# Two layers of gated cross-attention: the first layer's keys and queries as a seven-part block product

## The reference, cut to what matters

```python
x = _rmsnorm(hidden_states, ln_weight)
h_q = (x @ w_q.T).reshape(b, lq, H, DH)                     # H, DH = 32, 128; D = 512
h_k = (key_value_states @ w_k.T).reshape(b, lk, H, DH)
h_v = (key_value_states @ w_v.T).reshape(b, lk, H, DH)
score = jnp.einsum('bqhd,bkhd->bhqk', h_q, h_k)
score = score + position_bias[None]
score = jnp.where(m, score, -jnp.inf)
score = jax.nn.softmax(score, axis=-1)
attn = jnp.einsum('bhqk,bkhd->bqhd', score, h_v).reshape(b, lq, H * DH)
out = attn @ w_out.T
return hidden_states + out
```

## Time and profile before

| | |
|---|---|
| median of 3 runs | 1004.8 us (1004.76 to 1005.24) |
| the profiled execution | 1004.49 us, span 1002.7 us |
| TensorE busy | 995.0 us, 5204 matmuls |
| DVE, ACT, POOL busy | 466.8, 413.2, 336.4 us |
| one middle group (of 8) | 105.10 us |
| from the end of the last group to the end | 143.7 us |
| moved by DMA | 50.52 MB, mean 50 GB/s |

### The profile page before, as it was taken

The page is one execution under the profiler, slowest core; times in us unless marked ns, Lnnn a source line. Parts: engine busy times, 40 slices in busy tenths (PEclk is TensorE's granted clock), DMA queues, the critical chain, the costliest instruction groups (busy, mean ns, idle before and its releaser), DMA issues.

```text
span 1002.7 us, 14920 instructions
## 1 busy us (share of the span) xinstructions
PE 995.0 (99%) x5204; PEld 844.5 (84%) x5204; DVE 466.8 (47%) x957; ACT 413.2 (41%) x1110; POOL 336.4 (34%) x317
## 2 busy tenths in 40 slices
PE   8999999999999999999999999999999999999998
PEld 7888888888888888888888888888888888888885
DVE  5654622462155305532364235622462287766664
ACT  6563233432453244334442344234432454555630
POOL 3351414122330424041414051314122333587640
PEclk9999999999999999999999999999999999999999
DMA  8021111101110201010111011111101103300002
GB/s 312 22 84 55 42 43 64 32 21 63 42 52 0 84 28 55 10 63 21 63 31 63 21 63 31 42 42 63 31 21 64 42 2 99 122 33 1 1 1 84
DMA packets 16402, 50.52 MB, mean 50 GB/s; under 512 B 3056, under 2 KB 3312, under 8 KB 15600
## 3 DMA queue, kind: packets, MB, share of 16 engines
q1 hardware_dynamic: 15360, 48.75, 14.2%
q10 hardware_dynamic: 1008, 1.32, 0.4%
HBM read 47.97 MB, written 2.10 MB: 50 GB/s over the span
## 4 chain that ended last, share of the span: by engine, by line
PE 97%; DVE 1%; ACT 1%; POOL 1%; DMA 0%; issue 0%; SPq 0%; ACTq 0%; DVEq 0%
PE bank L1311 34%; PE bank L1369 17%; PE bank L1323 17%; PE bank L1430 10%; PE bank L1333 6%; PE bank L1353 6%; PE bank L1344 3%; PE bank L1423 2%; PE bank L1570 1%; PE bank L1507 1%; PE bank L1527 1%; POOL wvo L362 1%; DMA craw<-in_ctx 0%; DVE xt L891 0%; PE bank L1256 0%
## 5 line engine op out<-in xcount | busy, mean ns | idle before, releaser
L1311 PE MATMUL bank<-xt,wq 128*128 128x512 f32 x768 | 186.4, 393 | 0.0
L1311 PE MATMUL bank<-ct,wk 128*128 128x512 f32 x768 | 181.6, 392 | 0.7 <-DVE ct L857 0.7
L1369 PE MATMUL bank<-wvo,ao 128*128 128x512 f32 x768 | 180.6, 392 | 0.0
L1323 PE MATMUL bank<-wvo,ct 128*128 128x512 f32 x768 | 178.1, 390 | 0.2 <-POOL wvo L362 0.2
L1323 PEld LDWEIGHTS bank<-wvo,ct 128*128 128x128 f32 x768 | 143.4, 188 | 29.9 <-POOL wvo L362 0.6
L1311 PEld LDWEIGHTS bank<-ct,wk 128*128 128x128 f32 x768 | 142.7, 188 | 30.0 <-DVE ct L857 1.3
L1311 PEld LDWEIGHTS bank<-xt,wq 128*128 128x128 f32 x768 | 142.4, 188 | 29.1
L1369 PEld LDWEIGHTS bank<-wvo,ao 128*128 128x128 f32 x768 | 142.4, 188 | 28.6
L362 POOL TENSOR_TENSOR wk<-stage,wk 128x512 fp32r<-128x512 f32 x32 | 41.9, 1310 | 295.9 <-ACT wk L553 295.9
L362 POOL TENSOR_TENSOR wvo<-stage,wvo 128x512 fp32r<-128x512 f32 x64 | 81.7, 1306 | 162.3 <-ACT wvo L553 162.3
L569 ACT ACTIVATE prob<-prob,nmax 128x128 f32<-128x128 f32 x256 | 99.2, 389 | 61.5 <-DVE nmax L922 61.5
(11 more groups left out here) (148 smaller groups left out, 1120.1 us busy)
## 6 DMA issues: line engine op xcount, KB each, us to landing
stage<-in_w SPq DMA_DIRECT2D x63, 512.0 KB, 3.3
xraw<-in_x SPq DMA_DIRECT2D x2, 1024.0 KB, 12.5
bias<-in_bias SPq DMA_DIRECT2D x8, 256.0 KB, 2.7
cs<-in_ctx SPq DMA_DIRECT2D x1, 2048.0 KB, 9.2
out<-acc SPq DMA_DIRECT2D x8, 256.0 KB, 2.1
craw<-in_ctx ACTq DMA_DIRECT2D x4, 256.0 KB, 6.2
craw<-in_ctx SPq DMA_DIRECT2D x4, 256.0 KB, 6.5
stage<-in_w_key SPq DMA_DIRECT2D x1, 1024.0 KB, 4.8
```

The lines of the kernel that those rows point to most:

```text
L1311: mm = pe.matmul(bank[un_of[first][u] % RING][:, :], w[:, i, c, :], t[:, j, c, half(s)], start=(c == 0 and i + j == 0), stop=(c == KC - 1 ...
L1323: mm = pe.matmul(bank[un_of[first][u] % RING][:, :], ct[:, i, c, b * P:(b + 1) * P], wvo[:, j, c, :], start=(c == 0 and i + j == 0), stop= ...
L1369: mm = pe.matmul(bank[to][:, :], ao[:, h, i, b * P:(b + 1) * P], wvo[:, j, h, :], start=(h == heads[0] and i + j == 0), stop=(h == heads[- ...
```

## The change

Two heads (256 outputs) over 1024 tokens with a width of 512 are seen as a 2 x 2 by 2 x 2 block product: outputs in two heads, the width in two halves, the tokens in two halves. Instead of eight block products there are seven, P1 to P7, of 2 chunks x 3 passes = 6 matmuls each; their factors are single blocks or sums and differences of blocks, and the four result blocks are sums of products. In detail:

- The combinations of x and of the context (T1, T2, T3 and N4, two pieces of 512 KB each) are made once in group 0: DVE adds (`combine`), ACT and POOL split (`combined_hi`, `combined_lo`), SyncE stores them in device memory (`put`). They come back in pieces for each product (`fetch`) into a ring of seven places (`PLACE`); N4's second piece uses the place of T2's first.
- The weight combinations are made for each product: POOL subtracts and adds (`factors`), ACT rounds (`factors_hi`, `sums_hi`), POOL splits. There is one set of factors (`wkq`).
- ACT copies P1 out (`first_out`); DVE adds the other products to `qt` or `kt` in seven steps (`sums`, `STEPS`). Each now holds two heads.
- A group has four products: queries of heads 0 and 1, keys of 2 and 3, queries of 2 and 3, keys of 0 and 1 of the next group; the last group has three. Group 0 works plainly, and also makes keys 0 and 1 of group 1 (`plain`).
- `xt` goes, `ao` holds two heads; output is made in two rounds of two heads (`o0` to `o7`, `o8` to `o15`). The copy of the turned probabilities goes from DVE to ACT (`pt_out`). `bm` has one buffer, `stage` four rows instead of eight.
- In the last group the first three key tiles of the second layer stand between the output rounds.

```diff
-CHUNKS = ["k0", "q0", "v0", "v1", "v2", "v3", "k1", "q1", "o0", "o1", "o2", "o3", "k2", "q2", "k3", "q3"]
+CHUNKS = ["k0", "k1", "q0", "q1", "v0", "v1", "v2", "v3", "k2", "k3", "q2", "q3", "o0", "o1", "o2", "o3"]
...
+ORDER = ["P1", "P6", "P2", "P7", "P5", "P4", "P3"]
...
+BLOCK = {"P1": (0, 0), "P2": (1, 0), "P3": (1, 1)}
+COMBINED = {"P6": "T2", "P7": "T3", "P5": "T1", "P4": "N4"}
...
+PLACE = {"T2": (0, 1), "T3": (2, 3), "T1": (4, 5), "N4": (6, 0)}
...
+STEPS = ["u2", "C11", "u3", "C22", "u4", "C21", "C12"]
...
+ADDED = {"u2": "P6", "C11": "P2", "u3": "P7", "C22": "P5", "u4": "P5", "C21": "P4", "C12": "P3"}
...
+         "loop": seven(0) + VALUES[0:4] + seven(1) + VALUES[4:8] + seven(2) + OUTS[:B] + seven(3) + OUTS[B:],
+         "last": seven(0) + VALUES[0:4] + seven(1) + VALUES[4:8] + seven(2) + OUTS[:B] + ["t0", "t1", "t2"] + OUTS[B:]}
...
+                def fetch(z, t, c):
+                    sp.dma_start(ring[:, PLACE[t][c], :, :].bitcast(fp32), combined[z, TS.index(t), c, :, :, :]).then_inc(s_place[PLACE[t][c]], 16)
+
+                def last_piece(n, z):
+                    sp.wait_ge(s_prod, NPROD * n + AT["P6"])
+                    fetch(z, "N4", 1)
...
+                    last_piece(prods(g, 1), 0)
+                    second_piece(prods(g, 1), 1)
+                    other_pieces(prods(g, 1), 1)
...
+                        sp.wait_ge(s_flo, 3 * prods(g, 2) + 3)
+                        load(g + 1, "k0", 0)
+                    sp.wait_ge(s_vo_lo, vo_done(g, "loop", "o1"))
+                    load(g, "o2", 1)
+                    last_piece(prods(g, 2), 1)
+                    if last:
+                        return
+                    second_piece(prods(g, 2), 0)
+                    other_pieces(prods(g, 2), 0)
...
+                def body(g, last=False):
+                    vo_lo(g, "loop", "v2")
+                    vo_lo(g, "loop", "v3")
+                    biasmask(g, 0)
+                    factors(g, 1)
+                    biasmask(g, 1)
+                    factors(g, 2)
+                    vo_lo(g, "loop", "o0")
+                    vo_lo(g, "loop", "o1")
+                    biasmask(g, 2)
+                    if not last:
+                        factors(g, 3)
+                    vo_lo(g, "loop", "o2")
+                    vo_lo(g, "loop", "o3")
+                    biasmask(g, 3)
...
+                    first_out(g, m, 2)
+                    if last:
+                        act.wait_ge(s_spill, 32)
+                    ao_hi(g, 0)
+                    pt_out(g, 1)
+                    vo_hi(g, "loop", "o0")
+                    vo_hi(g, "loop", "o1")
+                    ao_hi(g, 1)
+                    exps(g, 2, range(2))
+                    if not last:
+                        factors_hi(g, 3)
+                        sums_hi(g, 3)
...
+                def product(g, m, j, p):
...
+                            at = PLACE[COMBINED[p]][c]
+                            if at:
+                                pe.wait_ge(s_place[at], 16 * n + 16)
+                            else:
+                                pe.wait_ge(s_place[0], 32 * n + (32 if p == "P4" else 16))
+                            right = lambda s: ring[:, at, s, :]
+                        for w, s in PASSES:
+                            mm = pe.matmul(bank[b][:, :], wkq[:, FACTOR[p], w, c, :], right(s),
+                                           start=(c == 0 and w + s == 0), stop=(c == 1 and w == 1))
...
+                    product(g, m, 2, "P1")
+                    attend(g, 0)
+                    product(g, m, 2, "P6")
+                    product(g, m, 2, "P2")
+                    transposes(g, 1)
+                    product(g, m, 2, "P7")
+                    product(g, m, 2, "P5")
+                    product(g, m, 2, "P4")
+                    attend(g, 1)
+                    product(g, m, 2, "P3")
+                    scores(g, m, 2)
```

More of the change, by code:

```diff
@@ new lines, in _ @@
+                vo_hi(0, "first", "v3")
+                plain_out("k0b")
+                for b in range(0, 4):
+                    context_squares(b)
+                plain_out("k1a")
+                for b in range(4, B):
+                    context_squares(b)
+                plain_out("k1b")
+                act.wait_ge(s_const, 32)
+                act.activation(tg[:, :], gates[:, :], ACT.Tanh).then_inc(s_a, 1)
+                plain_hi(2)
+                plain_hi(3)
+                for b in range(3):
+                    value_out(0, "first", b)
@@ new lines, in _ @@
+                for b in range(4):
+                    x_hi(b)
+                value_out(0, "first", 3)
+                for b in range(4, B):
+                    x_hi(b)
+                plain_hi(4)
+                for u in ("q0a", "q1a", "q0b", "q1b"):
+                    plain_out(u)
+                exps(0, 0, [0])
+                value_out(0, "first", 4)
+                exps(0, 0, [1])
+                plain_hi(5)
+                value_out(0, "first", 5)
+                combined_hi(0, 0, 0)
@@ L688, in normed @@
+                body(LAST, "last")
                 def normed(u, n):
@@ L1309, in proj @@
                             midway()
-                        for i, j in PASSES:
-                            mm = pe.matmul(bank[un_of[first][u] % RING][:, :], w[:, i, c, :], t[:, j, c, half(s)],
-                                           start=(c == 0 and i + j == 0), stop=(c == KC - 1 and i == 1))
-                    mm.then_inc(s_unit, 1)
-                def value(g, b, first):
+                        for p, j in PASSES:
+                            mm = pe.matmul(bank[un_of[m][u] % RING][:, :], wplain[:, i % 3, p, c, :],
+                                           block(c // 2, s)[:, j, c % 2, :],
+                                           start=(c == 0 and p + j == 0), stop=(c == KC - 1 and p == 1))
@@ new lines, in _ @@
+                pe.wait_ge(s_clo, HB)
+                plain("k0a", last_context)
+                pe.wait_ge(s_clo, B)
+                for u in ("k0b", "k1a", "k1b"):
+                    plain(u)
+                for b in range(3):
+                    value(0, "first", b)
+                for x in range(4):
+                    x_transposed(x)
+                value(0, "first", 3)
+                for x in range(4, B):
+                    x_transposed(x)
+                pe.wait_ge(s_xlo, 4 * KC)
@@ new lines, in _ @@
+                plain("q0a")
+                plain("q1a")
+                pe.wait_ge(s_xlo, B * KC)
+                plain("q0b")
+                plain("q1b")
+                scores(0, "first", 0)
+                for b in range(4, B):
+                    value(0, "first", b)
+                transposes(0, 0)
+                scores(0, "first", 1)
+                for u in PLAIN_UNITS[8:12]:
+                    plain(u)
+                plain("q2a")
+                attend(0, 0)
+                plain("q2b")
@@ new lines, in _ @@
+                transposes(0, 1)
+                plain("q3a")
+                attend(0, 1)
+                plain("q3b")
+                scores(0, "first", 2)
+                for i in range(6):
+                    project(0, "first", i)
+                transposes(0, 2)
+                scores(0, "first", 3)
+                project(0, "first", 6)
+                project(0, "first", 7)
+                attend(0, 2)
+                plain("k4a")
+                plain("k4b")
+                transposes(0, 3)
```

1264 lines of the change are left out of this document (816 added, 448 removed).

## The result

The changed kernel takes 1072.97 us (median, 1072.06 to 1074.64) where the kernel before takes 1004.78 in the same session: a ratio of 1.0679, 95% interval 1.0661 to 1.0698. It is slower, as forecast, but by 68 us and not by 21, and outside the range of 1000 to 1045.

The account below looks back on a forecast made before the run. TensorE, busy 99% of the span, was taken as the bound: 1004.5 - 36.7 + 39.9 + 5.4 + 7.2 + 5.4 = 1025.7 us, stated as 1025, range 1000 to 1045; slower was given 76%.

Parts of the forecast that it names:

- The gain: Key and query products: 1374 matmuls instead of 1536, 162 fewer at 0.2267 us each, -36.7 us.
- The last piece of product 2: Groups 1 to 7: its fetch stands behind a waiting load, so TensorE stalls 5.7 us in each, +39.9 us.
- pieces that compete: Rival, 9%: the fetch shares the DMA engines with six pieces around it; stall 12 us instead of 5.7, total 1069.
- The clock: Rival, 14%: TensorE's clock falls behind each of eight long stalls, 1.8 us lost each, +14, total 1040.
- From group 0 to 1: Combining ends at 122.3 us, before group 0's 131.6; stores and fetches then delay P4's data: +7.2 us (3 to 14).
- POOL and DVE: Rival: POOL's work stretches small DVE operations, softmax of heads 0 and 1 late by up to 2.4 us; no own chance.
- (a): Softmax of head 3 waits for POOL's later bias-mask sum, so transposes 3 wait: +0.9 x 6 = 5.4 us.
- The sum of DVE's new work per group: Middle group: DVE loses 8 copies and gains 28 additions from a bank, +13.6 us, to about 56 of some 100.
- Transposes of head 3: Six groups: DVE ends the second softmax_out at 83.8, transposes want it at 83.0: +0.9 us each, 5.4 together.
- The last group: Wait for layer 1's first key tile +2.4 us, and norm at the end +3.0: together +5.4 us (2 to 9).
- the key weights: Last group: layer 1's first key tile waits for POOL's splits, ready at 78.2 against 75.8: +2.4 us.
- the norm: End of last group: ACT's norm of tile 0 follows a rounding that waits for all output matmuls: +3.0 us.

Follow-up runs that it names:

- e7_both: e1_fetch plus, on POOL, the bias-mask sum of head 3 ahead of the splits of o2 and o3: 1007.25 us, ratio 1.0027 to the kernel before.
- e1_fetch: Changed kernel with SyncE fetching product 2's last piece ahead of the load of o2 and o3 in groups 1 to 7: 1020.28 us, ratio 1.0161.
- e3b_fill_half: Changed kernel with 22 small identity matmuls per group put into TensorE's wait for product 2's last piece: 1060.51 us, ratio 1.0552 to the kernel before.
- e4_alone: Separate kernel timing DVE and POOL operations alone and together, and TensorE batches behind waits: four DVE additions 4.63 us alone, 13.47 beside POOL.
- e5_none: Changed kernel with group 0's combining work run on 128 of 1024 columns, waits and DMA traffic kept: 1055.91 us.
- e8_group0: e7_both with group 0's combining work reordered on DVE, ACT and POOL, nothing left out: 995.66 us, ratio 0.9917 to the kernel before.

## Why the prediction was right or wrong

**The gain** (-36.7). Right: 1374 matmuls on keys and queries, and in e7_both a middle group of 99.96 us against 99.7.

**The last piece of product 2** (+39.9). Right in place, cause and nearly in size: 5.27 us, ended by DMA, once in each group, and its steps held too (the fetch issued 5.53 us after the transposes start, 5.55 reckoned; landed 4.2 us later, 4.35 reckoned). e1_fetch takes it away by the queue's order alone. The upper bound of 12 us (pieces that compete) did not show: the fetch landed 4.2 us after its issue.

**The clock.** Here the choice was wrong. I priced it rightly (1.8 us for each of eight waits, +14) and gave it 14%, with the argument that no row shows a fall of the column. But no row of a group before could: TensorE never waited in its groups. The one row that resembled a long wait, the cold start, spoke for it, and it should have been inside the forecast. e3b_fill_half gives 12.5 us for seven waits, and 109.15 - 101.66 - 5.27 = 2.2 us a group by e1_fetch. With it the forecast is 1040, still inside the range: this step alone didn't put the result outside.

The Trainium skill ("TensorE: Matmul & The Clock Gate", section "What's actually happening") says that an idle TensorE goes to 1.2 GHz; the granted clock of 0.50 behind the wait of 5.39 us in e4_alone agrees.

**From group 0 to 1** (+7.2, bounds 3 to 14). The step that failed: "20 combining operations ... go to DVE, and the last ends some 122.3 us into the span where TensorE's group 0 ends at 131.6". The last ended at 141.0 (139.77 + 1.23), and group 1 started at 152.1. Their own busy time is the small part of the error: 20 of them took 32 us against 27 reckoned. I summed DVE's work and compared ends, as if the combining were an addition beside the group's own work. In the list it stands in front of a softmax, of `ao_lo` and of additions that free banks, and each step's ACT and POOL part stands in front of others there. TensorE waited 15.3 us in five waits, mostly for those, and lost some 4 more at half pace: group 1 started 20.5 us late, which the term had put at nothing. e5_none gives the combining's share as 14.5 of these (17.1 us of the whole time), e8_group0 gets 11.6 us back by order. The wait for pieces that the term did price came out at 5.6 us in three waits against 7.2, in part by luck: the last combination and the end of group 0 were late together, and the distance between them stayed near 10 us. The middle group I had laid out instruction by instruction, and it held to 3%; group 0, where DVE had the most new work, I had not.

**POOL and DVE.** The rival named the mechanism, by a small operation stretched to the end of POOL's, and put it "inside (a)". It called that row a maximum; it is the change of sign behind it (`nmax<-rinv`), the form of the trial "four", while the maxima of e4_alone lost nothing. e4_alone shows that it is no matter of small operations but an exclusion: an addition of two SBUF tiles stands behind a whole POOL operation. The combining is 20 DVE operations of just this kind, with eight of POOL beside them.

The sum of DVE's new work per group is a little off: by its rows 28 x 0.683 less 8 copies of 0.645 is +14.0 and not +13.6; nothing hangs on it.

**Transposes of head 3** (+0.9 each). 1.25 measured. The order of POOL was the cause as reckoned: in e7_both 0.17 is left. The operations listed in (a) add up to 84.2 and not 83.8, a wait of 1.2. That it came out so near is partly luck, since the scaling of the probabilities took 1.70 us behind POOL's split where 0.69 are usual, and no term had that.

**The last group** (+5.4). The waits for the key weights (2.0 against 2.4) and the norm (2.5 against 3.0) are there. Missing were 3.0 us at the transposes of head 3, ahead of which this group has one key tile of 2.7 us where the others have five product parts of 1.36, and the clock: 1.8 to 2.2 us behind the ring's wait, 1.6 behind these transposes (12 matmuls in 4.11 us) and 1.6 behind the norm's wait (12 in 4.58). Less the 0.4, 0.5 and 0.6 by which the three reckoned waits were shorter, that is 6.5 to 6.9, against 6.4.

**The sum.** Of 47.6 us, group 0 is 20.5, the clock behind product 2's wait 12.5 to 15, group 1's first product 3.5, the last group's transposes 3.0 and its other half pace 3.2, 0.35 at the transposes and 0.2 at a bank in six groups 3.3, 7 x 0.4 for the shorter wait -2.8, and 0.9 for the last group's two other waits -0.9. That makes 42.3 to 44.8; the other 3 to 5 are spread over the groups and not divided further. Over two fifths of the error is the step that failed, group 0; over a quarter is the clock behind product 2's wait, which the forecast left out.

## What to carry to other kernels

Where TensorE never waits, price each new wait of several microseconds with what the clock takes behind it, about 2 us here, even if the old trace shows no fall; a wait near 2 us may cost it too. Work that is added to an engine with idle time is free only at its place in the list: lay out the stage in which it stands, softmax by softmax, not its sum. And before a fetch is put in a queue, look what the entry ahead of it waits for; two fetches put ahead of one waiting load in SyncE's list were worth 52.7 us, more than all the matmuls that the change took out (36.7).

## What the runs showed of the hardware

- DVE and POOL exclude each other where both add two float32 tiles in SBUF: 4 additions of 1024 columns take 4.63 us alone and 13.47 beside POOL's. A 4-column negation of one tile is held too, 0.155 alone and up to 2.38. Additions with a bank as operand (0.68), maxima of one tile (0.68), and additions beside a POOL fill (1.22) lose nothing. POOL loses too, 3.38 for 2.37.
- TensorE idle for 3.32 us loses 1.4 more, for 4.35 to 6.43 us 2.2 to 2.6, at a granted clock of 0.50 to 0.61 (e4_alone). After 2.28 us there it loses nothing, but in the kernels waits of 1.96 to 2.46 us are followed by either level: 12 matmuls behind 2.46 us take 4.58 us in the changed kernel and 3.00 in e7_both.
- A matmul on the float32 identity stands as two records of 0.11 us each for 128 columns.
